# Turning the layout in the stores between the cross and the attention part, with a new list of turns

## What is computed

```python
x = x + xattn(layernorm(x), ctx)      # causal self-attention, cross-attention to 257 keys, relu MLP
x = x + delta(layernorm(x))           # 2 layers: delta-rule attention, gated MLP
x = x + experts(layernorm(x))         # 32 routed experts, 8 chosen per token, and a shared one
```

## Time and profile before

| | us |
|---|---|
| median of 3 runs | 760.31 |
| lowest, highest | 758.68, 760.34 |
| profiled execution | 759.03 |
| its span, first to last instruction | 757.2 |
| TensorE (PE) matmuls busy | 619.0 |
| VectorE (DVE) busy | 461.9 |
| ScalarE (ACT) busy | 256.7 |
| GpSimd (POOL) busy | 97.0 |
| mean granted TensorE clock | 0.855 |

### The profile page before, as it was taken

One profiled execution on the slowest core, in us unless ns is written; L12 is line 12 of the kernel. 1 busy time (PEld: TensorE's weight loads), 2 busy tenths in 40 slices (PEclk: granted clock), 3 DMA queues, 4 the chain that ended last, 5 costly groups with the idle time before them and its releaser, 6 DMA issues.

```text
span 757.2 us, 15614 instructions
## 1 busy us (share of the span) xinstructions
PE 619.0 (82%) x6608; PEld 428.6 (57%) x6608; DVE 461.9 (61%) x1124; ACT 256.7 (34%) x555; POOL 97.0 (13%) x140
## 2 busy tenths in 40 slices
PE   2777951885789999695899599977888799999995
PEld 2534641575688869455698598776444344444442
DVE  5746594878966354747827843476556845555552
ACT  1455510653321623553642034204323132222221
POOL 2535452300000001201100001011011000000000
PEclk9888985855589999999758659976899999999998
DMA  9994021000000000000000041000032263333321
GB/s 345 298 368 165 1 81 31 0 2 2 2 3 3 3 1 3 0 2 1 2 2 3 1 121 60 1 3 0 1 84 62 64 164 86 97 97 111 88 80 28
DMA packets 18981, 46.68 MB, mean 62 GB/s; under 512 B 3456, under 2 KB 8192, under 8 KB 18656
## 3 DMA queue, kind: packets, MB, share of 16 engines
q1 hardware_dynamic: 18368, 45.43, 19.5%
q10 hardware_dynamic: 544, 0.26, 0.1%
HBM read 43.32 MB, written 2.36 MB: 60 GB/s over the span
## 4 chain that ended last, share of the span: by engine, by line
PE 64%; DVE 22%; ACT 5%; DMA 3%; POOL 2%; issue 2%; SPq 1%; DVEq 0%; POOLq 0%
PE psum L751 7%; PE psum L746 7%; PE psum L756 7%; PE psum L683 6%; PE psum L594 5%; PE psum L560 4%; PE psum L621 3%; PE psum L709 3%; PE psum L712 3%; PE psum L672 3%; PE psum L665 2%; PE psum L718 2%; PE psum L571 2%; DVE yr L1285 2%; DVE pcT L1285 2%
## 5 line engine op out<-in xcount | busy, mean ns | idle before, releaser
L930 ACT ACTIVATE arena<-psum 128x512 f32<-128x512 f32 x68 | 40.6, 598 | 134.8 <-PE psum L746 119.2
L1361 DVE TENSOR_TENSOR arena<-psum,arena 128x512 f32<-128x512 f32 x64 | 44.2, 691 | 59.2 <-PE psum L751 57.4
L756 PE MATMUL psum<-arena,wed_sb 128*128 128x512 f32 x128 | 66.3, 599 | 0.0
L774 ACT ACTIVATE arena<-psum 128x512 f32<-128x512 f32 x56 | 33.3, 601 | 70.8 <-PE psum L560 41.9
L1366 DVE TENSOR_TENSOR arena<-arena 128x512 f32<-128x512 f32 x64 | 44.3, 692 | 13.4 <-PE psum L756 13.2
L560 PE MATMUL psum<-arena 32*64 32x128 f32 x1024 | 44.4, 341 | 6.0 <-ACT arena L774 4.3
L950 POOL TENSOR_TENSOR ve<-ss,eps_rms 128x4 f32<-128x4 f32 x16 | 3.7, 229 | 337.3 <-ACT yr L825 249.4
L560 PEld LDWEIGHTS psum<-arena 32*64 32x64 f32 x1024 | 39.1, 173 | 12.2 <-ACT arena L774 5.6
L751 PE MATMUL psum<-yT,weu_sb 128*128 128x512 f32 x68 | 35.8, 609 | 8.3 <-DVE arena L1361 8.3
L756 PEld LDWEIGHTS psum<-arena,wed_sb 128*128 128x128 f32 x128 | 24.6, 192 | 31.1 <-issue 22.3
L1312 DVE TENSOR_TENSOR arena<-psum,small 128x1024 f32<-128x1024 f32 x24 | 28.2, 1216 | 14.2 <-PE psum L665 14.2
(11 more groups left out here) (283 smaller groups left out, 1281.7 us busy)
## 6 DMA issues: line engine op xcount, KB each, us to landing
arena<-shares SPq DMA_DIRECT2D x64, 256.0 KB, 3.9
arena<-in_ctx_t SPq DMA_DIRECT2D x16, 514.0 KB, 9.0
arena<-in_ctx_z SPq DMA_DIRECT2D x16, 512.0 KB, 10.8
XA<-in_x SPq DMA_DIRECT2D x1, 1024.0 KB, 4.9
zlast<-in_ctx_last SPq DMA_DIRECT2D x4, 256.0 KB, 17.0
x_mid<-XA SPq DMA_DIRECT2D x4, 256.0 KB, 3.0
weg_sb<-in_we_gate SPq DMA_DIRECT2D x2, 512.0 KB, 6.5
weu_sb<-in_we_up SPq DMA_DIRECT2D x2, 512.0 KB, 7.6
```

The source lines that it names most:

```text
L756: pe.matmul(x3, wed_sb[:, (p - 1) % (NPAIR + 1), :], act_a[pr], start=(p == 0), stop=False, skip_group_check=True).then_inc(x_down[pr], 1)
L774: return act.activation(out_, in_, ACT.Copy, scale=scale)
L930: act.activation(act_g[pr], banks[4 * pr + 2 * (n % 2)], ACT.Silu).then_inc(x_silu[pr], 1)
L1361: dve.tensor_tensor(act_gu[pr], banks[4 * pr + 1], act_g[pr], ALU.mult).then_inc(x_gu[pr], 1)
```

## The change

Three edits.

1. The stores turn the layout. `turned` stores 16 partitions of one group of XA with 4 runs of 512 bytes each to where X wants them in `x_mid`: 32 stores of 32 KB, of which ScalarE's queue issues 8. SP waits for all of them together and then loads X in two plain halves of 128 partitions, each with its own semaphore `x_home[pr]`, for which `ln` of that stream waits.
2. VectorE no longer waits for X ahead of the mask memsets, and in `n1` of layer 0 both groups are normed into `yn` before both are normed into `R`.
3. `TURNS` is another list of the same 246 letters, 123 of each stream.

```diff
-TURNS = ("AABAAABABABABBABAAABAABBAABABABABABBABAABAAAAAABAABABABBBBABAABAABABBABAAAABABABABABABABAABAABAA"
-         "BBABBABABABABABABABABABBABBBAABAAABBABBAABABABBABABBAABABABABBBBABAABAAABABAABBAABAABAABABABBABB"
-         "BBBBBAAABBBBABBABAABABBAABABABBBABBBABBABBBBAAABBABBAA")
+TURNS = ("AABAABAABAABBAABABABAABBAABAABABBAABAABBAAAAAAABBABABAABBABABAABABABAABAABABABBBABABABABAABAABAB"
+         "ABBABAAABBAABAABABABABABABABABABABABAAABBBBBBBBBABAAABBABBABBBBBABABBBAABAAABAABABABBBABBAABBA"
+         "BBBABAABABBBAABABABAAABBBAABAABAABBBABABBBABBAABBBABAB")
...
-        def home(g, a, s2):
+        def turned(g, a, s2):
 
             p0 = s2 * T + a * NJ + g * GT
-            return (X[p0:p0 + GT, :].rearrange("j (t d) -> j t d", d=D),
-                    gcols(x_mid, g)[a * S + s2:(a + 1) * S:2, :].rearrange("t (j d) -> j t d", d=D))
+            return (x_mid[p0:p0 + GT, :].rearrange("j (t d) -> t j d", d=D),
+                    gcols(XA, g)[a * S + s2:(a + 1) * S:2, :].rearrange("t (j d) -> t j d", d=D))
...
             for pr in range(2):
                 for u in range(NU):
-                    g = pr * NU + u
                     sp.wait_ge(x_done[pr], u + 1)
-                    sp.dma_start(gcols(x_mid, g), gcols(XA, g)).then_inc(x_out[u], 16)
-                for u in range(NU):
-                    sp.wait_ge(x_out[u], 16 * (pr + 1))
                     for a in range(NA):
                         for s2 in range(2 - pr):
-                            sp.dma_start(*home(pr * NU + u, a, s2)).then_inc(x_home, 16)
+                            sp.dma_start(*turned(pr * NU + u, a, s2)).then_inc(x_out, 16)
+            sp.wait_ge(x_out, 16 * 2 * NA * NG)
+            for pr in range(2):
+                half = slice(pr * NU * GW, (pr + 1) * NU * GW)
+                sp.dma_start(X[:, half], x_mid[:, half]).then_inc(x_home[pr], 16)
...
             for u in range(NU):
-                act.wait_ge(x_out[u], 32)
+                act.wait_ge(x_done[1], u + 1)
                 for a in range(NA):
-                    act.dma_start(*home(NU + u, a, 1)).then_inc(x_home, 16)
+                    act.dma_start(*turned(NU + u, a, 1)).then_inc(x_out, 16)
...
             dve.wait_ge(masks_made, 1)
-            dve.wait_ge(x_home, 16 * 2 * NA * NG)
             for m in range(C16):
                 last = dve.memset(below[:, m, :], 0.0)
...
                     if kind == "ln":
+                        dve.wait_ge(x_home[pr], 16)
...
-                        dve.wait_ge(d_rstd, i + 1)
-                        normed(lambda jj: gcols(X, g)[:, jj * D:(jj + 1) * D],
-                               lambda jj: gcols(R, g)[:, jj * D:(jj + 1) * D], g).then_inc(q_r, 1)
+                        if u == NU - 1:
+                            for k in range(NU):
+                                gk = pr * NU + k
+                                dve.wait_ge(d_rstd, gk + 1)
+                                normed(lambda jj: gcols(X, gk)[:, jj * D:(jj + 1) * D],
+                                       lambda jj: gcols(R, gk)[:, jj * D:(jj + 1) * D], gk).then_inc(q_r, 1)
```

More of the change, by code:

```diff
@@ L85 @@
 ROUTE = ["eln", "etr", "elog", "ro0", "ro1", "ro2", "ec"]
-TURNS = ("AABAAABABABABBABAAABAABBAABABABABABBABAABAAAAAABAABABABBBBABAABAABABBABAAAABABABABABABABAABAABAA"
-         "BBABBABABABABABABABABABBABBBAABAAABBABBAABABABBABABBAABABABABBBBABAABAAABABAABBAABAABAABABABBABB"
-         "BBBBBAAABBBBABBABAABABBAABABABBBABBBABBABBBBAAABBABBAA")
+TURNS = ("AABAABAABAABBAABABABAABBAABAABABBAABAABBAAAAAAABBABABAABBABABAABABABAABAABABABBBABABABABAABAABAB"
+         "ABBABAAABBAABAABABABABABABABABABABABABAAABBBBBBBBBABAAABBABBABBBBBABABBBAABAAABAABABABBBABBAABBA"
+         "BBBABAABABBBAABABABAAABBBAABAABAABBBABABBBABBAABBBABAB")
 def cross_schedule():
@@ L294, in perceiver @@
              "ca_read", "ff_up", "ff_h", "ff_out", "x_done"))
-        x_out = slots("x_out")
-        x_home, masks_made, d_steps = sem("x_home"), sem("masks_made"), sem("d_steps")
+        x_out, x_home = sem("x_out"), slots("x_home")
+        masks_made, d_steps = sem("masks_made"), sem("d_steps")
         d_var, d_rstd = sem("d_var"), sem("d_rstd")
```

## The result

| | before | after |
|---|---|---|
| median (4 runs each) | 759.49 us | 739.15 us |
| lowest, highest | 758.63, 760.34 | 738.10, 740.20 |
| profiled execution, its span | 759.03, 757.2 | 740.15, 738.4 |
| mean granted TensorE clock | 0.855 | 0.865 |

The account below looks back on a forecast made before the run. TensorE, busy 82% of the span, was taken to lose time at the DMA hand-over and in interleaving waits with half clock behind them. Hand-over -5.1 and list -11.3 made -16.4, from 760.31 to 743.9 us, range 732 to 758.

Parts of the forecast that it names:

- Stores of the hand-over: Cross part to attention part: turned stores issue in 0.466 us each, land by 115.6; statistics start at 119.5, 5.1 us less.
- the bounds of 1.5 and 6.1: Hand-over: 1.5 us less with stores at 80 GB/s and a load of 4.9 us, 6.1 less with a load of 2.8.
- the 122 that I had named as a sign of error: Hand-over: first statistics after 122 us would show the forecast wrong; near 119.5 us would show it right.
- the term that decides: Hand-over: how many DMA engines a transfer uses decides between the bounds; 4 for old loads, 16 for turned stores.
- Rival 3: Hand-over: the turned stores are no faster than the old loads, only 1.5 us less, 747.5 us; chance 0.10.
- Moved norms: n1 of layer 0: norms into R after both norms into yn; 0.1 us to gain, taken as 0.
- Layer 0 and layer 0 to 1: New list: 1 us less in layer 0's first half, 3 less where B's o covers A's sq and rs.
- Layer 1: New list: 5 us less around B's ext, 9 less at B's o, through fewer waits and o at full clock.
- Into the experts: New list: about 7.6 us of waiting ahead of B's etr, 4 back, some 3 of half clock; 6.5 us more.
- Rival 1: Whole list: only the hand-over pays, the new list trades stalls for equal ones; 755.2 us; chance 0.22.
- Rival 4: Layer 1: the clock stays up in both output stages and behind them, 8 us better, 736 us; chance 0.14.
- Rival 2: Experts: a 10 us wait ahead of B's etr, then half clock, makes it slower, about 765 us; chance 0.09.

Follow-up runs that it names:

- turns_only: The kernel before with the new list of turns alone, hand-over and norms as before: 742.77 us, ratio 0.981.
- fill_o: The kernel before with 14 unread matmuls ahead of TensorE's wait for o of stream B in layer 1: 759.99 us, ratio 1.002.
- experts_old: The changed kernel with the old list of turns from A's ro2 and B's mtr of layer 1 on: 737.34 us, ratio 0.973.

## Why the prediction was right, step by step

Forecast 743.9 us in a range of 732 to 758; measured 739.15. The direction and the main mechanism hold. The forecast was 4.8 us too slow. Of that, 2.5 lie in the profiled executions (742.6 forecast, 740.15 measured), and they are what is left of errors that partly cancel: 2.3 and 2.1 us too much hoped of the hand-over and the stretch behind it, 6.2 and 1.0 too little of the last two, and a cross part that ended 0.4 us later. The other 2.3 are the distance of the two profiled executions from the medians of their kernels, 1.3 of which I had added.

**Stores of the hand-over: issue mis-sized.** The step said 0.466 us a store from the output stores, last store at 113.9. Measured: 0.64 to 0.65 a store, and the last at 116.17. At that pace the 16 stores of the first pair, from 101.0 on, keep SP's queue until 111.3, and not until before 110 as I had it, and the 8 that follow end at 116.8. That queueing costs little by itself: ScalarE's queue, with nothing ahead of its 8, starts at 111.06 and ends at 116.48. Landing (1.9 us instead of 1.7) and load (4.03 instead of 3.8) were near. So the hand-over gave 2.8 us, between the bounds of 1.5 and 6.1, and the first statistics came at 122.22, just past the 122 that I had named as a sign of error. Of the 2.8, 1.3 are the memsets. The rule of the Trainium skill (DMA: Bandwidth & Descriptors, "Why a DMA increments its semaphore by 16 and not by 1"), on which I chose between the bounds, fits what is seen: while both queues store, the DMA share is above the 0.3 of the old loads:

```profile
113.00:114.00 1.00, 0.00 (x0) 0.00 (x0) 0.89 (x8) 0.00 (x0) 0.00 (x0) 0.50 0.47 107
```

The shares don't prove the number of engines, since the old loads' 0.32 is already above the 0.25 of four in sixteen. And it was not the term that decides, which I had said it was; the issue was. Rival 3 (1.5 us less) was nearer to the measured size than the forecast, for a reason that did not hold.

**Moved norms.** Predicted 0; the second yn starts at the word of GpSimd, as before, 4.8 us after the first statistics instead of 5.0. Right.

**Layer 0 and layer 0 to 1: predicted -4, measured -1.9.** The waits that I counted off did go (5.4 us less idle time), but 3.5 us of matmuls at half clock came in their place. I had charged nothing for the clock behind the new waits here.

**Layer 1: predicted -14, measured -20.2.** The two `o` stages gave the 5.9 and 6.2 us that I had read from the earlier trace rows. The term that was too small is the half clock around them: 17.6 us of matmul time went, where 12.1 less 3 was my sum; 12.1 are `o`, and 5.5 lie in the rest (`lout` 7.02 to 3.92 us is the largest row, and the work between B's `o` and `mtr` went from 11.7 to 7.7). The 3 us that I charged for half clock behind the new waits at B's `inv` were paid: behind the 4.03 us ahead of A's `mtr` the clock was at half until 443, and these matmuls took some 2.8 us more than at full clock, an estimate from rows of the same shapes.

```profile
436.00:440.00 4.00, 2.77 (x9) 1.96 (x10) 2.96 (x7) 1.19 (x2) 1.49 (x2) 0.51 0.01 2
```

So the term that was left out, half clock around the slow `o` stages, is about 8 us and not 5.5. The waits gave 2.6 us, where 2 and 3.9 less 1.1 was my sum: the new ones are as I had them (3.67 ahead of `lin`, 2 to 3 predicted; 4.03 ahead of A's `mtr`, 5 predicted), but of the 4.0 us that went from the matmuls between B's `o` and `mtr`, 2.4 came back as waits for VectorE and ScalarE.

**Into the experts: predicted +6.5, measured +5.7, and for another reason.** I had worked out 7.6 us of new waiting, less 4. The waiting fell by 1.1; all of the loss and more is clock (204.21 to 211.00 us of matmuls). The new waits are 2.17 and 3.17 us, since the matmuls of A between them take 3.7 us at half clock where I had 1.7. About 3 of the 5.7 us are the clock that was high by luck in the kernel before. The sum came out near by accident.

**Rivals.** Rival 1, that the list trades stalls for equal ones, falls with `turns_only`. Its half clock behind the wait at B's `inv` is real, but was over at 443, before `lout`. Rival 4, the clock stays up in both output stages and behind them (736 forecast), is what happened behind B's `o`; behind A's it fell again at the waits named above. Rival 2's mechanism, a wait ahead of `etr` and half clock, is there at 5.7 us of the 19 that it needed.

## What to carry to other kernels

Where a trace shows half clock behind a wait, cut the span into stretches with the same work and split each difference into TensorE's busy and idle time: here 17.6 of 20.2 us were the clock, and a wait of 3.9 us was worth 11. Price the clock with the wait, also in what follows the slow stage, and test it by unread matmuls that fill the whole of the wait; a fill that left 0.79 us open showed nothing, and one full fill showed the price. Before a low figure of a stretch is put down to the order, look for the same order in other runs: the clock behind the same wait differed, and with it 3 us. And price a DMA's issue from a row whose on-chip side has the same step between partitions, not only the same size.

## What had not been expected of the hardware

- On SP's queue a store from every second partition takes 0.64 us to issue, the same from neighbouring partitions 0.47; turning the layout on the DRAM side and doubling the bytes to 64 KB add nothing to it.
- Behind the same wait of 3.53 us in the same order of work the granted clock was 1.00 in the kernel before and 0.66 in `fill_o`.
- After 14 unread matmuls and 0.79 us of idle time the clock fell to 0.50 three microseconds into a run of small matmuls, on which TensorE was busy without a gap, and stayed there; after 20 and no gap it stayed at 1.00 through all of them.
- A stretch of unchanged program (`mtr` of B to the end, old order) took 224.1, 224.2, 227.1, 226.8 and 227.2 us in five kernels that differ only ahead of it; idle time was 19.5 to 19.9 us in before, `fill_o` and `experts_old`, and the difference is matmul time at a lower clock.
